# Expert results scattered with addition into the token rows instead of gathered at the end

## The reference

```python
x = x + mamba(xn) + moe(xn)

# moe
gate_logits = einsum('bsd,de->bse', x, gate_w) + gate_b
weights, indices = top_k(gate_logits, 2)          # 8 experts
weights = softmax(weights, axis=-1)
h = einsum('bsd,edh->ebsh', x, w1) + b1           # 256 -> 2 x 1024
act = silu(gh) * xh                               # the two halves of h
out_e = einsum('ebsf,efd->ebsd', act, w2) + b2    # 1024 -> 256
sum(out_e[picked] * weights, axis=2)
```

## Time and profile before

| | |
|---|---|
| time, median of 3 runs | 2693.53 us (2690.57 to 2693.56) |
| the profiled execution: its own time | 2695.5 us |
| its span in the trace | 2693.7 us |
| PE busy | 2148.6 us (80%) |
| DVE busy | 1952.0 us (72%) |
| ACT busy | 1374.4 us (51%) |
| POOL busy | 1155.9 us (43%) |
| DMA | 298.50 MB, mean 111 GB/s |
| stages, by first instruction | routing 739.2, mamba 764.8, experts 1882.9, combine 2595.4 us |

### The profile page before, as it was taken

The page is one execution under the profiler, slowest core; times in us unless marked ns, Lnnn a source line. Parts: engine busy times, 40 slices in busy tenths (PEclk is TensorE's granted clock), DMA queues, the critical chain, the costliest instruction groups (busy, mean ns, idle before and its releaser), DMA issues. The chain is left out here.

```text
span 2693.7 us, 34646 instructions
## 1 busy us (share of the span) xinstructions
PE 2148.6 (80%) x10642; PEld 1541.2 (57%) x10642; DVE 1952.0 (72%) x2745; ACT 1374.4 (51%) x2317; POOL 1155.9 (43%) x741
## 2 busy tenths in 40 slices
PE   2799999999836777887878787766799999999940
PEld 0577877777712323333323232323799999999940
DVE  6655555655421999898989898997688888888834
ACT  1332323333225766676757666632666666666620
POOL 1211222211215989989898989883000000000036
PEclk7899999999966999999999999999899999999975
DMA  6011001111011212222222222221655555655555
GB/s 245 16 40 39 12 27 39 39 39 39 27 43 54 100 59 100 80 91 76 98 76 100 82 89 84 82 96 38 264 220 209 209 214 224 226 221 210 196 164 164
DMA packets 115029, 298.50 MB, mean 111 GB/s; under 512 B 16820, under 2 KB 89540, under 8 KB 96148
## 3 DMA queue, kind: packets, MB, share of 16 engines
q1 hardware_dynamic: 108820, 280.97, 28.8%
q0 software_dynamic: 6144, 16.79, 1.9%
HBM read 247.45 MB, written 50.27 MB: 111 GB/s over the span
## 5 line engine op out<-in xcount | busy, mean ns | idle before, releaser
L1004 POOL TENSOR_TENSOR m_work<-m_ux,m_bb 128x1024 f32<-128x1024 f32 x256 | 598.5, 2355 | 22.2 <-DVE m_hh L1199 19.3
L1283 PE MATMUL m_y<-m_work,m_ident 128*128 128x512 f32 x1024 | 495.2, 606 | 1.5 <-DVE m_work L1205 1.5
L1144 ACT ACTIVATE m_da<-m_dl,m_A 128x512 f32<-128x512 f32 x512 | 348.3, 685 | 288.8 <-DVE m_hh L1199 288.0
L1768 POOL DMA_INDIRECT c_ya<-scratch_yg,c_dst x64 | 68.2, 1066 | 733.4 <-DMA c_wts<-scratch_wts 714.3
L1199 DVE TENSOR_TENSOR_SCAN m_hh<-m_da,m_work 128x512 f32<-128x512 f32 x256 | 298.4, 1207 | 107.6 <-POOL m_work L1004 107.0
L1699 PE MATMUL e_h<-e_xTh,e_w1h 128*128 128x256 f32 x1248 | 356.5, 286 | 16.8 <-DVE e_xTl L1635 16.8
L1699 PE MATMUL e_h<-e_xTh,e_w1l 128*128 128x256 f32 x1248 | 352.2, 282 | 0.0
L1699 PE MATMUL e_h<-e_xTl,e_w1h 128*128 128x256 f32 x1248 | 352.1, 282 | 0.0
L1205 DVE TENSOR_TENSOR m_work<-m_hh,m_cb 128x1024 f32<-128x1024 f32 x256 | 312.6, 1221 | 31.1 <-PE m_cb L1264 6.9
L1199 DVE TENSOR_TENSOR_SCAN m_hh<-m_da,m_carry,m_work 128x512 f32<-128x512 f32 x256 | 313.8, 1267 | 26.6 <-POOL m_work L1004 26.6
L1283 PEld LDWEIGHTS m_y<-m_work,m_ident 128*128 128x128 f32 x1024 | 198.6, 194 | 153.9 <-issue 141.7
(11 more groups left out here) (249 smaller groups left out, 4658.1 us busy)
## 6 DMA issues: line engine op xcount, KB each, us to landing
e_w<-in_w SPq DMA_DIRECT2D x39, 2048.0 KB, 7.5
m_bb<-scratch_bT SPq DMA_DIRECT2D x64, 1024.0 KB, 4.7
e_w<-in_w SPq DMA_DIRECT2D x39, 1024.0 KB, 9.5
e_xg<-scratch_xg SPq DMA_DIRECT2D x39, 256.0 KB, 9.6
scratch_yg<-e_yo SPq DMA_DIRECT2D x39, 256.0 KB, 9.7
scratch_xg<-x1p SPq DMA_DIRECT2D x19, 512.0 KB, 7.6
e_b<-in_b SPq DMA_DIRECT2D x39, 128.0 KB, 8.6
xt<-in_x SPq DMA_DIRECT2D x9, 512.0 KB, 5.6
```

The lines of the kernel that those rows point to most:

```text
L1004: pool.tensor_tensor(bx[:, u % NB], ux[q % 2][:, cols], slot.to_broadcast([P, HALF, T]), ALU.mult).then_inc(s_bx, 1)
L1144: act.activation(da[d % NA][:], dl[q % 2][:, e], ACT.Exp, scale=A[:, at:at + 1]).then_inc(s_exp, 1)
L1283: last = mm(y[:, i], ident[:], hc[:, u % 4, i], start=False, stop=(n % NST == NST - 1))
L1768: pool.indirect_dma_start(ya[:, a, :], None, dram["yg"][:, :], bass.IndirectOffsetOnAxis(ap=dst[:, a:a + 1], axis=0)).then_inc(yj[c], 16)
```

## The change

Each slot now has a record of REC = 260 values in the array `rec`, which replaces `xg`: the token's row (256) and four more (EXT): the row of `mo` that it belongs to (T + token), as an integer; the weight of the second pick; the difference of the weights of first and second pick; the expert of the first pick. `routing` writes these four per token to `ext`; `mamba` loads them beside the row and scatters all 260. `layer0` fills `rec` with zero records, whose row number is 0 to 255 (which are spare rows of `mo`, filled with zeros), in 40 DMAs.

In `experts` POOL takes the row numbers (`place`) and computes per slot the weight: the second's, plus the difference if the tile's expert is the token's first pick (`share`). An empty slot has weight 0. Then it multiplies `yo` by `share` and issues per tile two indirect DMAs that add 128 rows each to `mo` in DRAM (`compute_op=ALU.add`). It waits until the tile before has landed, so that two additions to one row don't overlap. The store to `yg` goes. SP loads the rows of tile t + 2 only when `share` of tile t is computed (`s_w`), which stands behind the landing of tile t - 2. `combine` only adds `x1p` and `mo`.

```diff
@@ layer0
-            sp_.wait_ge(s_zero, 1)
-            for at in range(0, NSLOT, T):
-                part = dram["xg"][at:min(at + T, NSLOT), :].rearrange("(s p) d -> p s d", p=P)
-                sp_.dma_start(part, zero[:, 0:part.shape[1]]).then_inc(zero_out, 16)
+            sp_.wait_ge(s_zero, 2)
+            sp_.dma_start(dram["mo"][0:S, :].rearrange("(s p) d -> p s d", p=P), empty[:, :, 0:D]).then_inc(zero_out, 16)
+            for t in range(NT):
+                sp_.dma_start(dram["rec"][t * S:(t + 1) * S, :].rearrange("(s p) d -> p s d", p=P), empty).then_inc(zero_out, 16)
...
-            pool.memset(zero[:], 0.0).then_inc(s_zero, 1)
+            pool.memset(empty, 0.0).then_inc(s_zero, 1)
+            pool.wait_ge(s_zero, 1)
+            pool.iota(empty[:, :, D].bitcast(I32), pattern=[[P, S // P]], base=0, channel_multiplier=1).then_inc(s_zero, 1)
@@ mamba
-                sp.dma_start(rows[:, j % 2], dram["xn1"][j * P:(j + 1) * P, :]).then_inc(rows_in[j % 2], 16)
+                sp.dma_start(rows[:, j % 2, 0:D], dram["xn1"][j * P:(j + 1) * P, :]).then_inc(rows_in[j % 2], 16)
+                sp.dma_start(rows[:, j % 2, D:REC], dram["ext"][:, j, :]).then_inc(rows_in[j % 2], 16)
...
-                pool.indirect_dma_start(dram["xg"][:, :], bass.IndirectOffsetOnAxis(ap=dst[:, at:at + 1], axis=0),
+                pool.indirect_dma_start(dram["rec"][:, :], bass.IndirectOffsetOnAxis(ap=dst[:, at:at + 1], axis=0),
@@ routing
+            pool.iota(ext[:, :, 0].bitcast(I32), pattern=[[P, NJ]], base=T, channel_multiplier=1).then_inc(s_c, 1)
...
-            sp.dma_start(dram["wts"], wts[:].rearrange("p k j -> p (k j)")).then_inc(s_out, 16)
+            sp.dma_start(dram["ext"], ext[:]).then_inc(s_out, 16)
...
+            step(dve.tensor_copy(ext[:, :, 1], wts[:, 1]), False)
+            step(dve.tensor_tensor(ext[:, :, 2], wts[:, 0], wts[:, 1], ALU.subtract), False)
+            step(dve.tensor_copy(ext[:, :, 3], pick[:, 0]), False)
+            dve.wait_ge(s_d, n[0])
@@ experts
+        def weigh(pool, t):
+            i = t % 2
+            pool.wait_ge(s_y, t + (Y0 + 1))
+            pool.wait_ge(s_w, t + (W0 + 1))
+            pool.wait_ge(s_place, t + 1)
+            pool.tensor_tensor(yo[i][:], yo[i][:], share[i][:].to_broadcast([P, NS, D]), ALU.mult).then_inc(s_yw, 1)
+            pool.wait_ge(s_yw, t + 1)
+            if t >= 1:
+                pool.wait_ge(y_out[1 - i], 16 * NS * ((t - 1) // 2 + 1))
+            for s in range(NS):
+                pool.indirect_dma_start(dram["mo"][:, :], bass.IndirectOffsetOnAxis(ap=place[i][:, s:s + 1], axis=0),
+                                        yo[i][:, s, :], None, compute_op=ALU.add).then_inc(y_out[i], 16)
+
         @block.gpsimd
         def _(pool):
             identity(pool, ident, s_id)
+            pool.wait_ge(texb_in, 16)
+            pool.tensor_copy(texf[:, :, 0], texb[:]).then_inc(s_texf, 1)
+            pool.wait_ge(s_texf, 1)
+            for t in range(NT):
+                i = t % 2
+                own = xg[i][:, :, D + 3:D + 4]
+                pool.wait_ge(x_in[i], 16 * (t // 2 + 1))
+                if t >= 2:
+                    pool.wait_ge(y_out[i], 16 * NS * (t // 2))
+                pool.tensor_copy(place[i][:], xg[i][:, :, D].bitcast(I32)).then_inc(s_place, 1)
+                pool.tensor_scalar(share[i][:], own, texf[:, t], None, ALU.is_equal).then_inc(s_share, 1)
+                pool.wait_ge(s_share, 2 * t + 1)
+                pool.tensor_tensor(share[i][:], share[i][:], xg[i][:, :, D + 2:D + 3], ALU.mult).then_inc(s_share, 1)
+                pool.wait_ge(s_share, 2 * t + 2)
+                pool.tensor_tensor(share[i][:], share[i][:], xg[i][:, :, D + 1:D + 2], ALU.add).then_inc(s_w, 1)
+                if t >= 1:
+                    weigh(pool, t - 1)
+            weigh(pool, NT - 1)
...
+            sp.dma_start(texb[:], dram["tex"].to_broadcast([P, NT])).then_inc(texb_in, 16)
...
                 sp.wait_ge(s_turn, t + 1)
-                sp.dma_start(xg[i][:], dram["xg"][bass.ds(t * S, S), :].rearrange("(s p) d -> p s d", p=P)).then_inc(x_in[i], 16)
+                sp.wait_ge(s_w, t + 1)
+                sp.dma_start(xg[i][:], dram["rec"][bass.ds(t * S, S), :].rearrange("(s p) d -> p s d", p=P)).then_inc(x_in[i], 16)
...
-            def store(t, i):
-                sp.wait_ge(s_y, t + (Y0 + 1))
-                sp.dma_start(dram["yg"][bass.ds(t * S, S), :].rearrange("(s p) d -> p s d", p=P), yo[i][:]).then_inc(y_out[i], 16)
...
@@ combine
-            sp.dma_start(dst[:], dram["dst"]).then_inc(small_in, 16)
-            sp.dma_start(wts[:], dram["wts"]).then_inc(small_in, 16)
...
             for c in range(NCH):
-                sp.wait_ge(s_y2, (c + 1) * SUB)
+                sp.wait_ge(s_add, c + 1)
                 sp.dma_start(out[c * T:(c + 1) * T, :].rearrange("(s p) d -> p s d", p=P), xa[:, c * SUB:(c + 1) * SUB]).then_inc(out_done, 16)
...
-                        pool.indirect_dma_start(ya[:, a, :], None, dram["yg"][:, :],
-                                                bass.IndirectOffsetOnAxis(ap=dst[:, a:a + 1], axis=0)).then_inc(yj[c], 16)
...
                 dve.tensor_tensor(xa[:, cs], xa[:, cs], mo[:, cs], ALU.add).then_inc(s_add, 1)
-                dve.wait_ge(s_add, c + 1)
-                dve.wait_ge(yj[c], 16 * SUB * TOPK)
...
-                        dve.scalar_tensor_tensor(out=xa[:, j], in0=ya[:, a], scalar=wts[:, a:a + 1], in1=xa[:, j],
-                                                 op0=ALU.mult, op1=ALU.add).then_inc(done, 1)
```

More of the change, by code:

```diff
@@ L63 @@
 TMAX = NTOK // S
+EXT = 4
+REC = D + EXT
 FMS = 4
 def layer0(nc, dram):
+    for name, shape in (("rec", (NSLOT, REC)), ("ext", (P, NJ, EXT))):
+        dram[name] = nc.dram_tensor("scratch_" + name, shape, F32, kind="Internal").ap()
     order = ([f"F{m}" for m in range(FMS)] + ["MS"] + [f"F{m}" for m in range(FMS, KH)]
@@ L157, in layer0 @@
         abs_f, abs_j = quad[:, 0:2 * KD], quad[:, 2 * KD:4 * KD]
-        zero = x1p
+        empty = x1p[:].rearrange("p s d -> p (s d)")[:, 0:S // P * REC].rearrange("p (s r) -> p s r", r=REC)
         carry = sb("carry", [P, KD])
@@ L263, in _ @@
             sp_.wait_ge(lg_out, 16)
-            sp_.wait_ge(zero_out, 16 * -(-NSLOT // T))
+            sp_.wait_ge(zero_out, 16 * (NT + 1))
             for s in (x1p_out, xn1_out, xrT_out):
@@ L818, in mamba @@
         bx, hc = work[:, 0:NB], work[:, NB:NB + 4]
-        rows = sb("rows", [P, 2, D])
+        rows = sb("rows", [P, 2, REC])
         hh = sb("hh", [P, 2, HALF, T])
@@ L1358, in _ @@
         def _(pe):
-            pe.wait_ge(s_c, 5)
+            pe.wait_ge(s_c, 6)
             pe.wait_ge(s_d, 2 * NJ + 1 + 1 + 1)
@@ L1424 @@
 SPLITS = 2 * KF
-D_STEPS = 2 * NJ + 3 + 3 + 1 + NE + 15
+D_STEPS = 2 * NJ + 3 + 6 + 1 + NE + 15
 PAIRS = KF // 2
 SPLITS = 2 * PAIRS
-D_STEPS = 2 * NJ + 3 + 3 + 1 + NE + 15
 def experts(nc, dram):
@@ L1456, in experts @@
         b2 = [sb(f"b2{i}", [P, D]) for i in range(2)]
-        xg = [sb(f"xg{i}", [P, NS, D]) for i in range(2)]
+        xg = [sb(f"xg{i}", [P, NS, REC]) for i in range(2)]
         xTh, xTl = ([sb(f"{n}{i}", [P, KD, S], F32R) for i in range(2)] for n in ("xTh", "xTl"))
@@ L1462, in experts @@
         yo = [sb(f"yo{i}", [P, NS, D]) for i in range(2)]
+        texb, texf = sb("texb", [P, NT], I32), sb("texf", [P, NT, 1])
+        place = [sb(f"place{i}", [P, NS], I32) for i in range(2)]
+        share = [sb(f"share{i}", [P, NS, 1]) for i in range(2)]
         tex_in, s_id = sem("tex_in"), sem("id")
+        texb_in, s_texf, s_place, s_share, s_w, s_yw = (sem("texb_in"), sem("texf"), sem("place"), sem("share"), sem("w"),
+                                                        sem("yw"))
         w_in = [sem(f"w_in{i}") for i in range(2)]
@@ L1552, in _ @@
                     load_rows(g * 2 + (4 + i), i)
-                    store(g * 2 + i, i)
                     load_b2(g * 2 + (2 + i), i)
@@ L1557, in _ @@
             load_rows(NT - 1, 0)
-            store(NT - 5, 0)
             load_b2(NT - 3, 0)
             load_b1(NT - 1, 0)
-            store(NT - 4, 1)
             load_b2(NT - 2, 1)
-            store(NT - 3, 0)
             load_b2(NT - 1, 0)
-            store(NT - 2, 1)
-            store(NT - 1, 0)
-            sp.wait_ge(y_out[0], 16 * ((NT + 1) // 2 + 1))
-            sp.wait_ge(y_out[1], 16 * (NT // 2 + 1))
+            sp.wait_ge(y_out[0], 16 * NS * ((NT + 1) // 2))
+            sp.wait_ge(y_out[1], 16 * NS * (NT // 2))
         @block.scalar
@@ L1621, in _ @@
             dve.sem_inc(s_turn, X0)
-            for i in range(2):
-                dve.sem_inc(y_out[i], 16)
+            dve.sem_inc(s_w, W0)
             def low(t, i, mm):
@@ L1736, in sem @@
             return ctx.enter_context(nc.semaphore("c_" + name))
-        dst = sb("dst", [P, NPICK], I32)
-        wts = sb("wts", [P, NPICK])
-        ya = sb("ya", [P, NPICK, D])
         xa = sb("xa", [P, NJ, D])
```

(25 more changed lines are left out.)

11 lines of the change are left out of this document (6 added, 5 removed).

## The result

The changed kernel takes 2626.51 us (median of four runs, 2626.02 to 2629.38) against 2692.05 (four runs, 2688.84 to 2693.56): a ratio of 0.976 with the interval [0.9743, 0.9777], 65.5 us saved, 2.4%. The profiled execution took 2626.03, its span is 2624.3; before it was 2693.7, so the two traces differ by 69.4. The forecast was 53.9 less, 2640, with a range from 2632: the kernel is faster than the whole range.

What follows compares the result with a forecast made beforehand. It took `combine`'s 64 POOL gathers as an exposed end piece, after a TensorE-bound expert stage. New tail, 2600.7, + 0.9 + 35.9 + 1.8 = 2639.3, plus 0.5 for small edits: span 2639.8, 53.9 less, time about 2640; range 2632 to 2661.

Steps and rivals of the forecast that it cites:

- Cost to the path: 0: Expert stage: added POOL work, waits and DMA fit beside TensorE, so a tile stays at 17.56 us.
- The cover: Expert stage: POOL's under 6 us fits in a 17.56 us tile; 7.7 us of further DMA time per tile is hidden.
- 0.5 later: Layer 0, routing and mamba stage: all small edits together were put at 0.5 us.
- Step 1, the tail: Expert stage's end: multiply, two scatters per tile and landings put `combine`'s first load at 2600.7, 4.4 us later than before.
- L = 4: Expert stage's tail: landing time of an accumulating scatter, taken as 4 us, between the plain scatter's 2.4 and 10.0.
- the step from landing to first load: Expert stage's end: from the last scatter's landing to SP's first load, 0.4 us, about one issue.
- Step 2, `combine`: End stage: 12.58 MB of loads and stores at full queues, 350 GB/s, 35.9 us, plus 0.9 start and 1.8 end.
- The rule against the cover: Expert stage: skill says POOL and two-SBUF-input VectorE instructions contend; forecast saw none in the trace, DVE having 3.0 us spare per tile.
- R1: Expert stage's tail: accumulating scatter takes 10 us to land even there, 12 later, about 2652; chance 0.08.
- R2: Mamba stage: its 64 scatters, with longer rows, take 0.2 us more each, 12.8 us, about 2653; chance 0.04.
- R3: Expert stage: accumulating rows hold the DMA engines and TensorE starves; at 6 us each, about 2770; chance 0.05.
- R4: End stage: additions are serialised, so it waits as long as for gathers; no net change, 2693; chance 0.02.

Runs made afterwards that it cites:

- e1: The kernel before with only 64 unused bytes per partition allocated behind `xg`: 2675.48 us against 2693.39, ratio 0.9931; tile 17.167.
- e2: The changed kernel with `xg` and `yo` exchanged in allocation order, so turned rows and activations lie as before: 2641.87 us, ratio 0.9808; tile 17.558.
- e3: The changed kernel with the addition left out of its scatters, so they only write: 2625.42 us in a single run; tile 17.167.
- e8: The changed kernel with `combine` merged into the expert stage's block, `x1p` loaded early: 2613.48 us against 2691.58, ratio 0.9704.
- e5: The changed kernel with 64 more unused bytes behind `xg` (128 against before): 2647.43 us in one run; tile 17.710.
- e4: The kernel before with only the new `combine` (16 loads, 8 additions, 8 stores), experts' results left out: 2633.2 us, ratio 0.9772; tile 17.56.

## Why the prediction was wrong, by its own steps

**The step that failed** stands in the part on the expert stage: "Cost to the path: 0", with the tile to stay at 17.56. The cover that this step was about held in every point, and the tile still changed. The new work is a multiply of 1.05 us, two scatters of 2.1 and four small operations per tile, and it costs TensorE nothing (e1 against after, before against e2: 0.00 us). The DMA time of the scatters was taken rightly too: 1.6 us per tile, and by POOL's queue (3.5% of the span, less 0.40 for each of the mamba stage's 64) it is 1.7. What the step left out is that a tensor which grows moves all that is allocated behind it. The diff showed it, `REC` in place of `D` in the allocation of `xg`, and I took it only for the bytes of a transfer. No row of the profile of before could have given the price; but TensorE at 99% busy with 0.122 us per matmul was taken as a constant, and it wasn't one. With the shorter tile the forecast of the profiled span, 2639.8, would have been 15.3 lower, where it missed by 15.5. That the rest then fits to 0.2 us is luck: the other terms' errors cancel.

The account of those 15.5 us, forecast against trace: the stage starts 3.2 earlier instead of 0.5 later, -3.7 (which isn't the change's doing); the stage -15.4; the tail +4.7; `combine` -1.1.

**Step 1, the tail**, was under-sized: 7.9 us forecast from the end of the last addition, 12.6 measured. L = 4 was right (the four scatters of the tail took 3.6 to 3.9 us to land). By the Trainium skill ("DMA: Bandwidth & Descriptors", section "Anatomy of one DMA") it was 2.3, from a formula that has no term for an addition: it holds for the plain scatter of e3, with 2.4, and not for the adding one. Two other terms were too small. The issues: 1.56 + 0.3 from start to start and not 1.3, and tile 37's landing awaited until 2577.78; the last issue stood 5.5 us after the addition, not 3.5. And the step from landing to first load, put at 0.4, is 3.2 by SP's waits: during 3.7 us nothing at all moves.

```profile
2583.00:2586.70 3.70, 0.00 (x0) 0.00 (x0) 0.00 (x0) 0.00 (x0) 0.00 (x0) 0.50 0.00 0
```

Waits of SP around it, in total, times and the longest: the landing first, then the block's end.

```profile
SPq L1444 <- DMA scratch_mo<-e_yo,e_place: 6.2, 1, 6.2
SPq L1444 <- PEq L1444: 3.2, 1, 3.2
```

Where the last work of a block is SP's own store, the gap is 0.4 (in the kernel before the last store is issued at 2592.81, lands 2.2 later, and SP goes on at 2595.39); where it is an indirect DMA of POOL it is 3.2 with the addition and 5.2 without (e3), and it falls away when the same SP queue goes on (e8). That it is tied to POOL's indirect DMAs is how these four cases lie; it was not taken apart further. Counted from POOL's last issue instead, the first load comes 7.1 us later in the changed kernel and in e2, 7.3 in e5 and 7.6 in e3, although the landing takes 3.6 in the first and 2.4 in the last. So the gap may well not begin at the landing at all, and then L of the last scatter has no part in the tail.

**Step 2, `combine`**, was right: 37.5 us against 38.6, at 348 to 376 GB/s where 350 was taken, and 37.9 in e4. The new end piece is a plain transfer at full queues.

**The rule against the cover.** I set the rule of the Trainium skill ("GPSIMD Engine Reference", section "Key points"), that POOL and a VectorE instruction with two SBUF inputs contend, against the earlier trace rows, and went by the rows: no contention. That was a misreading. Neither row tests the rule: L1628 has two SBUF inputs, but POOL was idle beside it, and of the inputs of L1205, which had a busy POOL beside it, `m_cb` lies in PSUM. The runs show the contention. DVE's `e_acl` addition (min/median/max), before, after, and in e2 with the addresses of before:

```profile
L1639 DVE TENSOR_TENSOR e_acl<-e_ac,e_ach x312: 411/415/426, 1911.4 to 2587.2; 128x256 fp32r<-128x256 f32 x156
```

```profile
L1674 DVE TENSOR_TENSOR e_acl<-e_ac,e_ach x312: 405/417/1096, 1908.0 to 2568.9; 128x256 fp32r<-128x256 f32 x156
```

```profile
L1674 DVE TENSOR_TENSOR e_acl<-e_ac,e_ach x312: 405/415/1093, 1907.8 to 2583.5; 128x256 fp32r<-128x256 f32 x156
```

One in eight takes 1.09 us. The timelines say which, POOL's and then DVE's:

```profile
2315.33 1.04 POOL L1515 TENSOR_TENSOR e_yo<-e_yo,e_share 128x512 f32<-128x512 f32 x1 [4.53 <-DVE e_yo L1680]
```

```profile
2315.56 1.09 DVE L1674 TENSOR_TENSOR e_acl<-e_ac,e_ach 128x256 fp32r<-128x256 f32 x1
```

It starts inside POOL's multiply, which reads SBUF, and ends 0.28 us behind it, so for most of the multiply it made no headway. By the Trainium skill ("SBUF — State Buffer", section "Who interferes with whom") the port pair that VectorE and GpSimd share is an exclusive lock, and a VectorE instruction with two SBUF inputs contends with a GpSimd instruction that reads SBUF; this trace agrees. It costs 0.67 us per tile on an engine that had 3.0 to give, so the sum would have been the same by the rule and by the row.

**The rivals.** R1: in mid stage the accumulating scatter does take up to 9.3 us to land, but in the tail 3.6 to 3.9; false. R2: L1013 takes 997 ns at the median, against 1008 before; false. R3: POOL waits 186.2 us for landings, but the loads of rows, issued at 2311.03 in the tile shown, stay inside their cover, and the DMA share rose only from 0.58 to 0.66; false. R4: the end piece takes 37.5 us from its first load instead of 97.4; false.

## What to carry to other kernels

Where an engine is busy 99% of the time, its pace is still a quantity to measure: when a change makes any buffer longer, compare the distance of two like instructions on that engine before and after, and try a pad of 64 bytes in the kernel before. It costs one line, and here it was worth 17.9 us alone and 15.4 within the change, about a quarter of what the whole change brought. Whether it helps another kernel can only be tried: at 128 bytes it made this one slower. A serial end piece that gathers may be replaced by accumulating scatters spread under a busy stage; what remains of it is the last tile's chain, issue, landing and the end of the block, and the last of these goes if the next stage's work follows in the same block. And before a row is held against a rule, its operands have to be those that the rule speaks of.

## What the hardware showed that I had not expected

- TensorE's time for a tile (144 matmuls of 256 columns, each with a new weight load, and the turning) is 17.16 to 17.71 us depending on the distance in SBUF between the split weights on one side and the turned rows and activations on the other (0, 64, 96, 128, 192 bytes more than before: 17.56, 17.17, 17.45, 17.71, 17.16). The Trainium skill ("SBUF — State Buffer", section "Who interferes with whom") gives the streamed operand and the weight load a read port each, independent of one another. By that alone the distance should not matter, and in these runs it does.
- An indirect DMA that adds takes POOL 1.55 us to issue and 3.6 to land at least, against 0.96 and 2.4 for the one that writes, and 96 packets more per 128 rows of 1 KB.
- Between the last landing of POOL's scatters and the first load of the next block lie 3.2 us (adding) and 5.2 us (plain) in which no engine and no DMA does anything.
- A VectorE addition of two SBUF inputs, 128x256, takes 0.42 us by itself and 1.09 when it starts inside a POOL multiply of 128x512.
